# Copies of packed queries and keys issued earlier on the SP queue, in a gated attention and mixture-of-experts layer

## The chip, the cores and the metric

The kernel runs on one core of one Trainium2 chip. The metric is the device time of one execution in microseconds. Three runs of the kernel before took 1435.66, 1438.06 and 1438.19 us; their median is 1438.06 us. The core has a TensorE (PE, matmuls), a VectorE (DVE), a ScalarE (ACT) and a GpSimd (POOL), which work side by side and wait for one another by semaphores, and SP, which here does nothing but issue copies (DMAs).

## The reference

The layer is a cross-attention with a gate, followed by a mixture of experts with a gate. The change is in the attention.

```python
# B=16 batches, N=256 tokens, M=1601 context rows, D=128, H=16 heads of 8
def _L0_xattn_ref(q, k, v, Wq, Wk, Wv, Wo):
    qh = jnp.einsum('bnd,hde->bhne', q, Wq)
    kh = jnp.einsum('bmd,hde->bhme', k, Wk)
    vh = jnp.einsum('bmd,hde->bhme', v, Wv)
    scores = jnp.einsum('bhne,bhme->bhnm', qh, kh) * SCALE
    att = jax.nn.softmax(scores, axis=-1)
    out_h = jnp.einsum('bhnm,bhme->bhne', att, vh)
    ...
x = x + jnp.tanh(g_xattn[0]) * _L0_xattn_ref(_layernorm(x), ctx_1024, ctx_1024, ...)
x = x + jnp.tanh(g_ffn[0]) * _L0_ffn_ref(_layernorm(x), ...)   # 8 experts, top 2
```

## The kernel before

The attention goes through the 16 batches, one after the other. A batch has 4 groups of 4 heads, and a group has 13 tiles of up to 128 context rows (the last has 65). One tile of one group is a *unit*; a batch has 52 units, r = 0 to 51, and every engine's program is written as a loop over all 832 units, in which r decides what is done besides.

In each unit TensorE makes the scores of its tile (L716, `st`), ScalarE takes their exponentials (L1022), and TensorE multiplies those of two units ago with the values (L759, `pv`). The softmax needs the maximum of each query's scores beforehand. For that TensorE computes the scores a second time in *windows* of 402 context rows (L738, `mxp`), VectorE reduces each window (L1456, `mx`), GpSimd splits the maxima in three bf16 terms (L610 to L616), TensorE turns them (L773), ScalarE copies them to `mxT` (L1077), and SP copies them into three rows of `qpack` (L427, `place_maxima`). From there the matmul of the scores subtracts them. The windows run ahead: at the start of a batch 28 of its 64 windows are done, and the first window of the *next* batch is issued in unit 27.

Queries and keys are float32, but are multiplied as bf16: each number is split into three bf16 terms (`qsp`, `ksp`), and six products of terms are stacked in the rows of `qpack` and `kpack`. The stacking is what SP's copies do:

- `pack_queries(b)` (L379) is 12 copies of 32 KB: 6 parts, each for 2 row groups;
- `pack_keys(b, g)` (L373) is 12 copies of 50 KB for one group of heads, so 48 a batch.

`qpack` and `kpack` each have two halves; batch b uses half b % 2. So the packs of batch b + 1 wait until all scores of batch b - 1 are done (`s_st`), and until the terms are there (`s_q3`, `s_k3`).

SP's program is one queue: what stands behind a wait or behind other copies goes later. In the loop of batch b it holds, in this order of units: 9 (maxima of group 1; queries of b + 1; keys of b + 1, group 0), 23 (maxima of group 2; keys of groups 1 and 2), 35 (maxima of group 3; keys of group 3; load of a context), 48 (maxima of group 0 of the next batch). SP itself does not follow the units. It runs on to its next wait, and the only waits of the loop that hold it for long are those for `mxT`.

At the turn of two batches GpSimd issues the four scatters of token rows for the experts (L644, `write_rows`), and TensorE begins with the key projection of the next batch (L818, in units 1, 2, 3 and 6). Values are projected in units 13, 14, 27 and 32 (L827). After the last batch come the experts: 39 blocks of 256 tokens, whose results are scattered by GpSimd (L652).

Of the kernel before, what the change touches and what calls it, by code (L numbers as in the profile page):

```python
# [16 lines left out]
B, N, D = 16, 256, 128  # L17
# [32 lines left out]
PARTS = len(K_KIND)  # L50
# [140 lines left out]
def build(nc, x, ctxT, gates, wq, wk, wv, woT, rwT, w1T, w2T, ident, tables, pads, out):  # L191
# [4 lines left out]
    with ctx:  # L196
# [173 lines left out]
        def pack_key_rows(eng, b, g, part, rg):  # L370

            p0 = rg * RSTEP
            eng.dma_start(kpack[p0 + part:p0 + MAXROW:PARTS, b % 2, g * JJ:(g + 1) * JJ, 0:M],  # L373
                          ksp[p0 + g:p0 + RSTEP:NG, K_KIND[part], 0:M]
                          ).then_inc(s_kd[b % 2][g], 16)

        def pack_query_rows(eng, b, part, rg):
            r = rg * RSTEP
            eng.dma_start(qpack[r + part:r + MAXROW:PARTS, b % 2, :, :],  # L379
                          qsp[r:r + RSTEP, Q_KIND[part], :]).then_inc(s_qd[b % 2], 16)  # L380
# [16 lines left out]
        def _(eng):  # L397
# [5 lines left out]
            def pack_keys(b, g, kinds=range(PARTS)):  # L403

                if g == 0:
                    eng.wait_ge(s_k3, NK * (b + 1))
                    if b > 1:
                        eng.wait_ge(s_st, RG * UNITS * (b - 1))
                for part in kinds:
                    for rg in range(RG):  # L410
                        pack_key_rows(eng, b, g, part, rg)

            def pack_queries(b):
                eng.wait_ge(s_q3, b + 1)
                if b > 1:
                    eng.wait_ge(s_st, RG * UNITS * (b - 1))
                for part in range(PARTS):
                    for rg in range(RG):
                        pack_query_rows(eng, b, part, rg)

            def place_maxima(G):
                b, g = divmod(G, NG)
                eng.wait_ge(s_mxT, G + 1)
                rows = KINDS * JJ
                for rg in range(RG):
                    r = rg * RSTEP + MAXROW
                    eng.dma_start(qpack[r:r + KINDS, b % 2, g * JJ:(g + 1) * JJ, :],  # L427
                                  mxT[rg * rows:(rg + 1) * rows, :]).then_inc(s_mxd[G % 2], 16)

            def load_context(b):  # L430
                if b + 2 < B:
                    eng.wait_ge(s_v, NV * (b + 1))
                    eng.dma_start(ctx_sb[:, b % 2, :], ctxT[b + 2]).then_inc(s_ctx[b % 2], 16)
# [22 lines left out]
            for u in range(B * UNITS):  # L456
                b, r = divmod(u, UNITS)
                if u == 20:
                    eng.dma_start(rows[NE * CAP:NE * CAP + SPARE * SL, :], pads[NE * 2 * SL:PADS, :]
                                  ).then_inc(s_pad, 16)  # L460
                if r in PLACE_AT and b * NG + PLACE_AT[r] < GROUPS:
                    place_maxima(b * NG + PLACE_AT[r])
                if b == 0:
                    if r == 9:
                        pack_queries(1)
                    elif r == 23:
                        pack_keys(1, 0)
                        pack_keys(1, 1)
                    elif r == 35:
                        pack_keys(1, 2)  # L470
                        pack_keys(1, 3)
                        load_context(1)
                elif b + 1 < B:
                    if r == 9:
                        pack_queries(b + 1)
                        pack_keys(b + 1, 0)
                    elif r == 23:
                        pack_keys(b + 1, 1)
                        pack_keys(b + 1, 2)
                    elif r == 35:  # L480
                        pack_keys(b + 1, 3)
                        load_context(b + 1)
# [1215 lines left out]
```

## Time and profile before

| | |
|---|---|
| median of 3 runs | 1438.06 us (1435.66 to 1438.19) |
| the profiled execution | 1438.06 us, its span 1436.2 us |
| granted TensorE clock, mean | 0.966 |
| TensorE, VectorE, ScalarE, GpSimd busy | 93%, 82%, 77%, 38% |
| SP's key packs, query packs, maxima | 762, 186 and 128 copies |
| one batch of the attention | about 74 us |

The profile is that of one execution. A page gives the busy time of each engine, the chain of work that ended last, and groups of instructions by line. Queries of the trace behind it give, for a stretch of time, every instruction of an engine, what it waited for, and the share of time for which the DMA engines were busy. Names are those of the program: `qpack<-qsp` is a copy from `qsp` to `qpack`. An engine's idle time counts only if the engine is on the chain that sets the end.

### The profile page before, as it was taken

Reading aid. Unit: us, or ns where it says so; the run is one execution under the profiler, and the core shown is the slowest. Engines: PE = TensorE matmul, PEld = TensorE weight load, DVE = VectorE, ACT = ScalarE, POOL = GpSimd, SP = SyncE. Lnnn points to the kernel's source line nnn. Section 1 sums busy time; section 2 is a strip of 40 time slices with the busy share of each in tenths; the row PEclk is TensorE's granted clock in tenths of the full one; section 3 lists DMA queues with packets and bytes.
Section 4 is the critical chain, followed back from the end, with each engine's and each line's share of the span. In section 5 each row is a group of like instructions: output and inputs, shape, how many; then the busy total and the mean of one; then the engine's idle time right before and its main releaser. Section 6 shows DMA issues by size and latency. Waiting matters only on the chain.

```text
span 1436.2 us, 37917 instructions
## 1 busy us (share of the span) xinstructions
PE 1339.1 (93%) x13936; PEld 651.0 (45%) x13936; DVE 1171.2 (82%) x2302; ACT 1100.8 (77%) x2202; POOL 545.2 (38%) x1213
## 2 busy tenths in 40 slices
PE   4689999999999999999999999999999999998993
PEld 2233444444444444444444443434444433486882
DVE  6777898989898989898989898989999998253444
ACT  1467898888888979797988888888888888764551
POOL 1231525262625253435353535343434312144442
PEclk7698999999999999999999999999999999899996
DMA  3422121212121212121212121212111110375665
GB/s 87 149 65 63 30 77 38 77 36 78 33 81 28 74 35 71 38 69 42 67 44 65 47 64 50 62 52 56 59 53 38 49 43 2 108 226 173 205 208 197
DMA packets 65556, 109.15 MB, mean 76 GB/s; under 512 B 13452, under 2 KB 36364, under 8 KB 65228
## 3 DMA queue, kind: packets, MB, share of 16 engines
q1 hardware_dynamic: 56716, 92.46, 21.9%
q0 software_dynamic: 4544, 9.45, 2.0%
q10 hardware_dynamic: 4112, 4.83, 1.0%
q8 instruction: 111, 1.82, 0.5%
q14 instruction: 73, 0.60, 0.1%
HBM read 48.81 MB, written 14.64 MB: 44 GB/s over the span
## 4 chain that ended last, share of the span: by engine, by line
PE 80%; DVE 10%; issue 3%; another core or an unknown queue 2%; SPq 1%; DMA 1%; ACT 1%; ACTq 1%; POOL 0%; POOLq 0%; DVEq 0%
PE pv L759 28%; PE mxp L738 15%; PE st L716 14%; DVE mx L1456 9%; PE st L983 5%; PE mxp L993 5%; PE st L827 4%; PE st L818 3%; PE st L838 2%; SPq L373 1%; PE st L790 1%; PE st L861 1%; PE st L802 1%; ACT arena L1022 1%
## 5 line engine op out<-in xcount | busy, mean ns | idle before, releaser
L1456 DVE TENSOR_REDUCE mx<-mxp 128x2 f32<-128x804 f32 x1024 | 987.5, 989 | 118.7 <-PE mxp L738 81.9
L1022 ACT ACTIVATE arena<-st 128x512 f32<-128x512 f32 (+1 forms) x1664 | 898.6, 594 | 145.9 <-PE st L716 118.6
L759 PE MATMUL pv<-arena 128*32 128x256 f32 x6656 | 538.2, 395 | 12.9 <-issue 12.2
L738 PE MATMUL mxp<-kpack,qpack 48*128 48x402 bf16 x2048 | 455.5, 344 | 34.4 <-DVE mx L1456 20.6
L716 PE MATMUL st<-qpack,kpack 51*128 51x256 bf16 (+1 forms) x3328 | 459.3, 274 | 11.3 <-issue 10.2
L716 PEld LDWEIGHTS st<-qpack,kpack 51*128 51x128 bf16 (+1 forms) x3328 | 207.2, 97 | 216.7 <-ACT arena L1022 110.6
L738 PEld LDWEIGHTS mxp<-kpack,qpack 48*128 48x128 bf16 x2048 | 139.5, 94 | 177.9 <-DVE mx L1456 85.8
L759 PEld LDWEIGHTS pv<-arena 128*32 128x32 f32 x6656 | 132.5, 108 | 191.4 <-issue 100.2
L610 POOL CAST mxs<-nmx 128x8 bf16<-128x8 f32 x64 | 12.1, 189 | 323.1 <-DVE nmx L1464 323.1
L1162 ACT ACTIVATE arena<-st,bias 128x256 f32<-128x256 f32 x156 | 73.5, 474 | 64.2 <-PE st L983 43.3
L652 POOL DMA_INDIRECT results<-ysb,idx x78 | 74.8, 959 | 106.3 <-DVE ysb L1588 93.8
L983 PE MATMUL st<-xT,arena 128*128 128x256 f32 x312 | 94.9, 387 | 6.5 <-ACT xT L1150 6.1
L644 POOL DMA_INDIRECT rows<-xrow,pos x64 | 63.9, 998 | 92.4 <-DVE pos L1345 77.4
L536 POOL TENSOR_TENSOR tmp<-rstd 128x2 f32<-128x2 f32 x93 | 18.0, 193 | 208.1 <-DVE rstd L1218 203.2
L993 PE MATMUL mxp<-arena 128*128 128x256 f32 x312 | 93.9, 384 | 0.0
L1588 DVE TENSOR_SCALAR ysb<-mxp,xblk,tgate 128x128 f32<-128x128 f32 x78 | 28.4, 405 | 48.2 <-PE mxp L967 44.0
L818 PE MATMUL st<-arena,wk_sb 128*128 128x400 f32 (+1 forms) x126 | 62.0, 578 | 5.2 <-DMA arena<-in_ctxT 5.2
L993 PEld LDWEIGHTS mxp<-arena 128*128 128x128 f32 x312 | 60.1, 193 | 8.4
L827 PE MATMUL st<-wv_sb,arena 128*128 128x128 f32 (+1 forms) x416 | 62.2, 289 | 0.0
L827 PEld LDWEIGHTS st<-wv_sb,arena 128*128 128x128 f32 (+1 forms) x416 | 49.6, 187 | 25.1 <-issue 24.6
L983 PEld LDWEIGHTS st<-xT,arena 128*128 128x128 f32 x312 | 53.6, 193 | 12.0 <-ACT xT L1150 6.7
L585 POOL TENSOR_TENSOR ksp<-kf,ksp 128x400 bf16<-128x400 f32 (+1 forms) x60 | 56.8, 947 | 4.8
(183 smaller groups left out, 976.6 us busy)
## 6 DMA issues: line engine op xcount, KB each, us to landing
kpack<-ksp SPq DMA_DIRECT2D x762, 50.0 KB
arena<-in_ctxT SPq DMA_DIRECT2D x15, 800.5 KB, 4.4
arena<-in_w1T SPq DMA_DIRECT2D x39, 256.0 KB
arena<-in_w2T SPq DMA_DIRECT2D x39, 256.0 KB
qpack<-qsp SPq DMA_DIRECT2D x186, 32.0 KB
xblk<-rows SPq DMA_DIRECT2D x39, 132.0 KB
rows<-in_pads SPq DMA_DIRECT2D x8, 264.0 KB
qpack<-mxT SPq DMA_DIRECT2D x128, 3.0 KB
```

What stands on the lines that cost most here:

```text
L644: eng.indirect_dma_start(rows, bass.IndirectOffsetOnAxis(ap=pos[:, k, t:t + 1].bitcast(U32), axis=0), xrow[:, t, k, :], None).then_inc(don ...
L652: eng.indirect_dma_start(results, bass.IndirectOffsetOnAxis(ap=idx[:, i % IDX_BUFS, j:j + 1].bitcast(U32), axis=0), ysb[:, i % YS_BUFS, j, ...
L716: ins = eng.matmul(ring[i][0:n, jj * N:(jj + 1) * N], kpack[rows, b % 2, g * JJ + jj, kt * P:kt * P + n], qpack[rows, b % 2, g * JJ + jj, ...
L738: eng.matmul(mxp[pair % MX_BUFS][:, rg, 0:WIN], qpack[rows, b % 2, g * JJ + jj, t * P:(t + 1) * P], kpack[rows, b % 2, g * JJ + jj, WSTART ...
L759: ins = eng.matmul(pv[32 * j:32 * j + 32, 0:N], vaug[0:n, b % 2, kt, VC * h:VC * h + 32], pt[0:n, (2 * u + rg) % PT_BUFS, jj * N:(jj + 1) ...
L818: eng.matmul(dst[:, 0:kn], wk_sb[:, :], ctx_sb[:, b % 2, k0:k0 + kn], start=True, stop=True).then_inc(s_kp, 1)
L827: ins = eng.matmul(ring[i][0:n, t * D:(t + 1) * D], ctx_sb[:, b % 2, (t0 + t) * P:(t0 + t) * P + n], wv_sb[:, :], start=True, stop=True)
L983: eng.matmul(hp[q % HP_BUFS][:, 0:SL], wbuf[:, i % W_BUFS, 0, c * P:(c + 1) * P], xT[:, i % 2, :], start=True, stop=True).then_inc(s_hp, 1)
L993: eng.matmul(yp[i2 % 2][:, 0:SL], wbuf[:, i2 % W_BUFS, 1, c2 * P:(c2 + 1) * P], hf[:, f % RING, :], start=(c2 == 0), stop=(c2 == HC - 1)). ...
L1022: eng.activation(pt[0:n, c % PT_BUFS, :], ring[bank_of["S", u, p]][0:n, :], ACT.Exp, scale=SCALE).then_inc(s_exp, 1)
L1162: eng.activation(hf[:, q % RING, :], hp[q % HP_BUFS][:, 0:SL], ACT.Gelu_apprx_tanh, bias=bias[:, i % BIAS_BUFS, c:c + 1]).then_inc(s_hg, 1)
L1456: eng.tensor_reduce(mx[:, tj, w, :], mxp[windows_done % MX_BUFS][:, :, 0:WIN], AX.X, ALU.max).then_inc(s_red, 1)
```

## The change

In the loop of SP the query packs of the next batch move from unit 9 to unit 1, which also puts them ahead of the maxima of group 1. This holds for the batches b = 1 to 14; batch 0 keeps its order. The twelve key packs of group 1 are cut in two: the first three parts (6 copies) are issued at unit 16, the other three at unit 23 as before. No other engine's program changes, and no wait is added or removed; the waits of `pack_queries` move with it.

```diff
@@ -458,6 +458,8 @@
                 if u == 20:
                     eng.dma_start(rows[NE * CAP:NE * CAP + SPARE * SL, :], pads[NE * 2 * SL:PADS, :]
                                   ).then_inc(s_pad, 16)
+                if r == 1 and 0 < b < B - 1:
+                    pack_queries(b + 1)
                 if r in PLACE_AT and b * NG + PLACE_AT[r] < GROUPS:
                     place_maxima(b * NG + PLACE_AT[r])
                 if b == 0:
@@ -472,10 +474,11 @@
                         load_context(1)
                 elif b + 1 < B:
                     if r == 9:
-                        pack_queries(b + 1)
                         pack_keys(b + 1, 0)
+                    elif r == 16:
+                        pack_keys(b + 1, 1, range(PARTS // 2))
                     elif r == 23:
-                        pack_keys(b + 1, 1)
+                        pack_keys(b + 1, 1, range(PARTS // 2, PARTS))
                         pack_keys(b + 1, 2)
                     elif r == 35:
                         pack_keys(b + 1, 3)
```

On SP's queue before, one batch of the steady state stands as follows, from the context load at the end of one batch to the next. The first row `qpack<-mxT` is the maxima of group 0 and of group 1.

```order
L433 DMA arena<-in_ctxT 128x1601
L427 DMA qpack<-mxT 3x2x256 x4
L379 DMA qpack<-qsp 8x8x256 x12
L373 DMA kpack<-ksp 8x2x1601 x12
L427 DMA qpack<-mxT 3x2x256 x2
L373 DMA kpack<-ksp 8x2x1601 x24
L427 DMA qpack<-mxT 3x2x256 x2
L373 DMA kpack<-ksp 8x2x1601 x12
```

The same stretch of SP's queue in the changed kernel:

```order
L433 DMA arena<-in_ctxT 128x1601
L427 DMA qpack<-mxT 3x2x256 x2
L379 DMA qpack<-qsp 8x8x256 x12
L427 DMA qpack<-mxT 3x2x256 x2
L373 DMA kpack<-ksp 8x2x1601 x18
L427 DMA qpack<-mxT 3x2x256 x2
L373 DMA kpack<-ksp 8x2x1601 x18
L427 DMA qpack<-mxT 3x2x256 x2
L373 DMA kpack<-ksp 8x2x1601 x12
```

The query packs now stand between the maxima of group 0 and those of group 1, and the 12 and 24 key packs around the maxima of group 2 have become 18 and 18.

## Rows read from the trace of the kernel before

**Rows 1.** The page, part 1: busy time of each engine.
```profile
PE 1339.1 (93%) x13936; PEld 651.0 (45%) x13936; DVE 1171.2 (82%) x2302; ACT 1100.8 (77%) x2202; POOL 545.2 (38%) x1213
```
**Rows 2.** The page, part 4: the chain that ended last, by engine.
```profile
PE 80%; DVE 10%; issue 3%; another core or an unknown queue 2%; SPq 1%; DMA 1%; ACT 1%; ACTq 1%; POOL 0%; POOLq 0%; DVEq 0%
```
**Rows 3.** Tile qpack: releaser of its matmuls, us idle in total, times.
```profile
  DMA qpack<-mxT: 2.7, 6
```
**Rows 4.** Waits: engine, line, releaser, total us, times, longest us.
```profile
PE mxp L738 <- DMA qpack<-qsp: 8.6, 1, 8.6
```
**Rows 5.** Timeline of SP from 520 us: start, us, line, copy, count.
```profile
526.68 1.43 SPq L427 DMA_DIRECT2D qpack<-mxT  x2
528.22 7.90 SPq L379 DMA_DIRECT2D qpack<-qsp  x12
536.22 7.79 SPq L373 DMA_DIRECT2D kpack<-ksp  x12
...
546.08 1.51 SPq L427 DMA_DIRECT2D qpack<-mxT  x2
547.64 15.67 SPq L373 DMA_DIRECT2D kpack<-ksp  x24
```
**Rows 6.** Stretches: us, engines' busy time, PEclk, DMA share, GB/s.
```profile
512.00:515.00 3.00, 2.06 (x19) 0.93 (x18) 0.34 (x2) 1.33 (x4) 2.34 (x4) 1.00 0.18 58
...
528.00:536.00 8.00, 8.00 (x94) 4.46 (x95) 7.04 (x16) 6.37 (x13) 0.00 (x0) 1.00 0.18 45
...
545.00:547.60 2.60, 2.60 (x35) 1.40 (x27) 2.44 (x4) 2.14 (x5) 0.00 (x0) 1.00 0.01 1
```
**Rows 7.** Timeline of TensorE at the batch's turn and in unit 27.
```profile
508.27 0.27 PE L716 MATMUL st<-qpack,kpack 51*65 51x256 bf16 x1
...
553.05 0.34 PE L738 MATMUL mxp<-kpack,qpack 48*128 48x402 bf16 x2
```
**Rows 8.** Timeline of GpSimd: the query terms, first and last of four scatters.
```profile
500.64 0.67 POOL L598 TENSOR_TENSOR qsp<-qf,qsp 128x256 bf16<-128x256 f32 x1
...
509.02 1.10 POOL L644 DMA_INDIRECT rows<-xrow,pos  x1 [5.46 <-DVE pos L1345]
...
512.97 0.97 POOL L644 DMA_INDIRECT rows<-xrow,pos  x1 [0.30 <-issue]
```
**Rows 9.** Timeline of VectorE: idle us and releaser in brackets.
```profile
514.80 1.90 DVE L1456 TENSOR_REDUCE mx<-mxp 128x2 f32<-128x804 f32 x2 [2.66 <-remote]
```
**Rows 10.** The chain in order of time at the start of batch 6: start, us.
```profile
512.14 2.68 another core or an unknown queue
```
**Rows 11.** Timeline of SP: the maxima of group 0, start of a period.
```profile
283.34 22.25 SPq L427 DMA_DIRECT2D qpack<-mxT  x4
...
356.78 22.99 SPq L427 DMA_DIRECT2D qpack<-mxT  x4
...
430.98 22.99 SPq L427 DMA_DIRECT2D qpack<-mxT  x4
```
**Rows 12.** Timeline of ScalarE and SP: mxT and the late maxima of batch 5.
```profile
487.95 0.36 ACT L1077 ACTIVATE mxT<-st 12x256 bf16<-12x256 f32 x1
...
489.97 1.51 SPq L427 DMA_DIRECT2D qpack<-mxT  x2
...
526.30 0.36 ACT L1077 ACTIVATE mxT<-st 12x256 bf16<-12x256 f32 x1
```
**Rows 13.** Timeline of TensorE's weight loads: waits for maxima, batches 5, 10.
```profile
492.59 0.09 PEld L716 LDWEIGHTS st<-qpack,kpack 51*128 51x128 bf16 x1 [0.41 <-DMA qpack<-mxT]
...
863.19 0.09 PEld L716 LDWEIGHTS st<-qpack,kpack 51*128 51x128 bf16 x1 [0.58 <-DMA qpack<-mxT]
```
**Rows 14.** The page, parts 2 and 5: DMA by slices; scatters, mean ns.
```profile
DMA  3422121212121212121212121212111110375665
...
L652 POOL DMA_INDIRECT results<-ysb,idx x78 | 74.8, 959 | 106.3 <-DVE ysb L1588 93.8
L644 POOL DMA_INDIRECT rows<-xrow,pos x64 | 63.9, 998 | 92.4 <-DVE pos L1345 77.4
```

## The prediction

> **What bounds the kernel now.** I read the busy shares first [rows 1]: TensorE has work for 93% of the span, VectorE for 82%, ScalarE for 77%. The chain of waits [rows 2] agrees: 80% of the span is TensorE's, 10% VectorE's, and DMA and the SP queue have 1% each. So the span is set by TensorE, and the change touches only the order in which SP issues copies. It can matter in three ways: a wait of a computing engine on one of those copies goes or comes; a copy behind them on SP moves; or the copies meet other traffic at a bad place. I went through them in this order.
>
> First, who waits for the copies at all. The tile view of qpack and the table of waits answer: over the whole run TensorE was idle 2.7 us in six waits for the maxima [rows 3], and once, for 8.6 us, for query packs [rows 4]. A wait that comes once in 16 batches is that of the start, where nothing runs ahead, and the packs of batch 0 are not moved. No wait for kpack stands in either view.
>
> Second, how late the packs are. Batch 6 (from about 509 to 583 us) stands for the steady state. SP issues the 12 query packs from 528.22, the first 12 key packs from 536.22 to 544.01 [rows 5]. From 545.0 on the DMA share is 0.01 [rows 6], so the last key pack of group 0 has landed by about 545.5. The first window of the next batch is the matmul at 553.05, behind the value projection of L827 [rows 7]. The slack is 7.5 us before the change.
>
> Third, what else happens at the place to which the query packs go. On SP the packs will stand behind the group-0 maxima, and then wait for the last scores of the batch before. Those are the 65-row matmuls that end at 508.54 [rows 7]. So the packs will be issued from about 508.6. In exactly that stretch GpSimd issues four scatters of token rows, 509.02 to 513.94 [rows 8], and in exactly that stretch all three computing engines stand still: VectorE waits 2.66 us [rows 9], and the chain has 2.68 us of "another core or an unknown queue" [rows 10]; from 512 to 515 VectorE works 0.34 us and ScalarE 1.33 us [rows 6]. Batches come in two lengths, and this stop is where they differ. From the SP rows: 356.78 - 283.34 = 73.44 us and 430.98 - 356.78 = 74.20 us [rows 11], 0.76 us apart. By the same rows nine of the batches 2 to 14 are of the long kind and four of the short one. This is the only part of the loop where I find anything to win or to lose.
>
> **The change part by part.** The profiled execution took 1438.06 us (span 1436.2, 1.9 us around it). That is the median of the three runs as well, so the sum is made against 1438.06.
>
> (a) Query packs of batches 2 to 15 move from unit 9 to unit 1 of the batch before, ahead of the maxima of group 1. Twelve packs with their gaps take 7.90 us [rows 5]: 508.6 + 7.9 = 516.5. The next copy on SP is the group-1 maxima, issued at 526.68 right behind mxT at 526.30 + 0.36 [rows 5, 12]. SP is free 10 us before that, so this copy is not delayed: cost 0. The new wait on s_st stands in front of the same copy only, and is over at 508.54: cost 0. The split queries it reads are finished by GpSimd at 500.64 + 0.67 [rows 8]. What the packs free later: the first key packs go from 536.22 to about 528.2, and slack grows from 7.5 to 15.5 us. It was not used, so 0.
>
> (b) Half of the group-1 key packs (3 of 6 parts, each for two row groups, so 6 of 12 copies) go ahead of the maxima of group 2: 6 x 0.65 = 3.9 us. With (a) SP runs 528.2 + 7.8 + 3.9 = 540 us, and the group-2 maxima are due at 546.08 [rows 5]. 6 us of slack, cost 0. Without (a) the six would end at 548 and push the maxima by 2 us; (a) is the cover of (b).
>
> (c) Behind the group-2 maxima stand now 18 packs instead of 24: 18 x 0.653 = 11.8 us instead of 15.67. The group-3 maxima are free to go at 547.64 + 11.8 = 559.4 and wait for mxT instead of for SP. In a batch such as batch 5, SP took 16.44 us for the 24 and issued the maxima at 489.97, while mxT was there at 487.95 + 0.36 = 488.31: 1.66 us late [rows 12]. TensorE's weight load then names this copy, but it is idle 0.41 us there, which is what it is idle in the neighbouring units as well; only in batch 10 is it 0.58 [rows 13]. The gain is 0.58 - 0.41 = 0.17 us once. The bound from above is the whole 2.7 us of [rows 3].
>
> (d) The last twelve key packs and the context load of each batch go earlier by at most 15.67 - 11.8 = 3.9 us. Nobody waits for either: 0.
>
> (e) The meeting with the scatters. No row of before shows the two together in the loop. Bounds: below, that the stop becomes short everywhere, 9 batches x 0.76 us = -7 us. Above: the query packs hold the DMA engines for a share of 0.18 over 8 us [rows 6], 1.44 us of each engine; if the stop grew by all of that in the 13 batches that have both, +18.7 us. The nearest rows speak for a value near 0: the scatters of the tail (results), issued where the last digits of the page's DMA line show 30 to 79% busy, take 959 ns on GpSimd; those of the loop (rows), with next to no other traffic, 998 ns [rows 14]. I take 0.
>
> The Trainium skill ("DMA: Bandwidth & Descriptors", section "Issuing engines are not separate DMA queues") says that copies started by sync and by gpsimd run on the same 16 DMA engines and interleave, whoever starts them. That rule speaks against this change, which puts twelve packs onto the engines that have to carry the scatters; that the scatters wait for it is not shown by any run here. By it the sum would be the rival below, 1444; by the GpSimd durations it is the forecast.
>
> Sum: 1438.06 - 0.17 + 0 = **1437.9 us**.
>
> **The rivals.**
> Rival 1, slower: the scatters' data wait behind the packs, and the stop that ends with them grows. Twelve packs hold each engine 1.44 us, 0.12 us each on the mean; four scatters that each meet one add 0.5 us to the stop, in 13 batches 6 us: 1444. For it: the stop lies exactly under the scatters, in a batch with scatters and with nothing else on the queues (DMA share 0.18 between 512 and 515 [rows 6]). Against it: the GpSimd durations above. It decides from 0.22 us per batch.
>
> Rival 2, faster: the stop is short instead of long. Long and short batches start with the same order, so something small decides; a shift by the packs may bring all to the short kind: 1438.06 - 7 = 1431. Against: nothing says that the shift goes this way.
>
> Rival 3, the reverse: the four short batches become long, 4 x 0.76 = +3: 1441.
>
> Rival 4, the change does not do what it says: the packs "at unit 16" follow the packs of unit 9 on SP with no wait between, so nothing is held until unit 16, and the time is the forecast's.
>
> **How the numbers follow.** What a measurement can tell from no change here is about 0.2%, 2.9 us. Forecast (with rival 4) 0.48, own range 1436 to 1440. Rival 1 0.24, rival 2 0.17, rival 3 0.11. Rival 2 is faster by over 0.2%, with 0.05 of the forecast's case that the stop shifts partly to the short kind: faster 0.22. Rival 1 in all and half of rival 3 are slower: 0.30. Same is the rest, 0.48. The 8-in-10 range takes in rival 2, rival 3 and most of rival 1: 1431 to 1446.
>
> **What would show it.** (a) SP's query packs at the start of each batch, 20 us before the group-1 maxima, and these right behind mxT. (b), (c) 18 packs on either side of the group-2 maxima, the group-3 maxima always right behind mxT, and no six waits of L716 on them. (e) The stop: VectorE's idle time before the windows behind the scatters (2.66 us in batch 6) and the batch periods of 73.4 and 74.2 us. If the periods are the old two in about the old numbers, the forecast is right for its reason. If all are 74.6 and over it is rival 1, if all are 73.4 rival 2. The forecast would be wrong too if the first windows of a batch (L827 ahead of them) waited for DMA, or if the maxima of group 1 were issued later than mxT.

## The result, and the profile after

The changed kernel took 1470.88 us (median of 4 runs, 1470.43 to 1476.03); the kernel before took 1438.12 us (median of 4, 1435.66 to 1441.16). The ratio is 1.0235, 95% interval 1.0205 to 1.0265: the change made the kernel slower by 33 us. The forecast was 1437.9 us, its range ended at 1446.

The profiled execution of the changed kernel was its fastest: 1459.57 us, span 1457.8 us, mean granted clock 0.954. The other four ran at 0.946 to 0.949. So the trace shows 21.5 us of the loss, against 1438.06 us of before. The run of 1470.63 us lost 11 us more; its clock (0.949 over a span of 1468.8 us) accounts for at most 7.8 us of them.

The page after, part 1 and the chain by engine of part 4 (they answer to [rows 1, 2]):

```profile
PE 1354.1 (93%) x13936; PEld 653.0 (45%) x13936; DVE 1171.7 (80%) x2302; ACT 1103.3 (76%) x2202; POOL 548.0 (38%) x1213
...
PE 82%; DVE 9%; issue 3%; another core or an unknown queue 3%; DMA 1%; ACT 1%; ACTq 1%; POOL 0%; POOLq 0%; SPq 0%; DVEq 0%
```

The instruction counts are the same. The span grew by 1457.8 - 1436.2 = 21.6 us. TensorE's busy time grew by 1354.1 - 1339.1 = 15.0 us, that is, the same matmuls took longer; the other 6.6 us are time in which it stood. The granted clock bears this out: 1457.8 x (1 - 0.954) - 1436.2 x (1 - 0.966) = 18.2 us of the full clock were lost in addition, which is the most that the clock can have cost. VectorE's busy time did not grow (1171.2 before).

SP, changed kernel: start, us, line, copy, count. The first rows are the turn to batch 5.

```profile
286.81 7.90 SPq L379 DMA_DIRECT2D qpack<-qsp  x12
...
361.40 7.90 SPq L379 DMA_DIRECT2D qpack<-qsp  x12
...
432.50 1.51 SPq L427 DMA_DIRECT2D qpack<-mxT  x2
436.01 7.90 SPq L379 DMA_DIRECT2D qpack<-qsp  x12
457.00 1.52 SPq L427 DMA_DIRECT2D qpack<-mxT  x2
458.63 11.76 SPq L373 DMA_DIRECT2D kpack<-ksp  x18
...
513.14 7.90 SPq L379 DMA_DIRECT2D qpack<-qsp  x12
587.74 9.12 SPq L379 DMA_DIRECT2D qpack<-qsp  x12
```

The queue does what the order said: the query packs at the turn, 18 key packs in a piece where 12 and 24 stood. The packs also mark the batches, since they wait for the last scores of the batch before: 74.59, 74.61, 77.13 and 74.60 us from one to the next. Before, the two lengths were 73.44 and 74.20 [rows 11]. So these batches are 0.4 us longer than the old long kind, and one is 2.9 us longer.

Where that is: at the turn, under the scatters. GpSimd, VectorE and the chain of the changed kernel at the turn to batch 5 (start, us, then the instruction, with its idle us and their releaser in brackets; the chain has start, us, and what held it):

```profile
436.36 1.11 POOL L647 DMA_INDIRECT rows<-xrow,pos  x1 [5.46 <-DVE pos L1348]
...
440.32 0.97 POOL L647 DMA_INDIRECT rows<-xrow,pos  x1 [0.31 <-issue]
```

```profile
438.56 0.99 DVE L1459 TENSOR_REDUCE mx<-mxp 128x2 f32<-128x804 f32 x1 [0.57 <-PE mxp L741]
442.56 1.90 DVE L1459 TENSOR_REDUCE mx<-mxp 128x2 f32<-128x804 f32 x2 [3.01 <-remote]
...
449.52 1.00 DVE L1459 TENSOR_REDUCE mx<-mxp 128x2 f32<-128x804 f32 x1 [2.35 <-PE mxp L741]
```

```profile
439.30 1.76 another core or an unknown queue
...
441.20 1.26 another core or an unknown queue
...
443.05 1.70 PE st L821 x2
```

The scatters are as long and as far apart as before [rows 8] (509.02 to 512.97 there, 436.36 to 440.32 here: 3.95 and 3.96 us). VectorE's wait in the middle of them is 3.01 us instead of 2.66 [rows 9], the nameless piece of the chain 1.76 + 1.26 = 3.02 us instead of 2.68 [rows 10]. TensorE had computed the window by then:

```profile
439.39 0.56 PE L741 MATMUL mxp<-kpack,qpack 48*128 48x402 bf16 x4
...
441.57 0.64 PE L762 MATMUL pv<-arena 128*32 128x256 f32 x8 [1.25 <-issue]
```

```profile
439.00:442.00 3.00, 1.75 (x18) 0.60 (x16) 0.55 (x1) 1.18 (x3) 1.94 (x2) 1.00 0.42 103
442.00:445.00 3.00, 2.15 (x10) 0.63 (x6) 2.14 (x4) 1.69 (x4) 1.79 (x3) 0.64 0.25 63
445.00:449.00 4.00, 4.00 (x23) 1.52 (x20) 1.90 (x2) 1.74 (x4) 3.55 (x9) 0.50 0.02 6
```

TensorE works 1.75 us of 3, then 2.15 of 3, and then the granted clock is at 0.50, the lower of its two levels (1.2 GHz), while it works without a pause: 23 matmuls in 4 us, with VectorE (1.90) and ScalarE (1.74) half idle behind it. That is the second wait of 2.35 us at 449.52. In the changed kernel's trace this happens behind the turn of eight batches (5, 9 to 15); in the one of before it happens at no turn of batches 2 to 15.

Measured from first scatter to first scatter, batches 2 to 14 take 982.51 us together, against 959.97 before, 22.5 us more. The six batches without a fall (2 to 4, 6 to 8) have 3.6 us of this, 0.6 us each; the seven with one (5, 9 to 14) have 18.9 us. The eighth fall, at the turn to batch 15, comes where no query packs are issued, behind a VectorE wait of 1.26 us, and the stretch from there to the next scatters is only 0.5 us longer than before.

Two stretches of 15 us over a turn, with the fall (batch 5) and without it (batch 8), both from some 2 us ahead of the first scatter:

```profile
434.00:449.00 15.00, 12.90 (x107) 4.75 (x100) 8.99 (x15) 8.91 (x18) 9.36 (x15) 0.79 0.18 46
660.00:675.00 15.00, 12.76 (x132) 4.74 (x124) 10.93 (x17) 10.88 (x22) 9.19 (x15) 1.00 0.18 46
```

TensorE is as busy in both, and gets 107 matmuls done in the one and 132 in the other.

### The profile page after: what moved, and what is told of

It is laid out like the page before. It is cut to its first block, busy times and chain, and to the rows that moved or that the text cites. A ratio compares the mean times of both kernels' runs of the same rounds, so it can differ in the third digit from the quotient of the medians.

```text
span 1457.8 us, 37917 instructions
## 1 busy us (share of the span) xinstructions
PE 1354.1 (93%) x13936; PEld 653.0 (45%) x13936; DVE 1171.7 (80%) x2302; ACT 1103.3 (76%) x2202; POOL 548.0 (38%) x1213
## 4 chain that ended last, share of the span: by engine, by line
PE 82%; DVE 9%; issue 3%; another core or an unknown queue 3%; DMA 1%; ACT 1%; ACTq 1%; POOL 0%; POOLq 0%; SPq 0%; DVEq 0%
PE pv L762 29%; PE st L719 15%; PE mxp L741 15%; DVE mx L1459 8%; PE st L986 5%; PE mxp L996 4%; PE st L830 4%; PE st L821 4%; PE st L841 2%; PE st L793 1%; DMA arena<-results 1%; PE st L864 1%; PE st L805 1%; PE mxp L962 1%
## 5 line engine op out<-in xcount | busy, mean ns | idle before, releaser
L741 PE MATMUL mxp<-kpack,qpack 48*128 48x402 bf16 x2048 | 461.6, 348 | 29.0 <-DVE mx L1459 14.4
L986 PE MATMUL st<-xT,arena 128*128 128x256 f32 x312 | 94.4, 386 | 6.1 <-ACT xT L1153 5.7
L647 POOL DMA_INDIRECT rows<-xrow,pos x64 | 64.1, 1001 | 92.3 <-DVE pos L1348 77.4
L821 PE MATMUL st<-arena,wk_sb 128*128 128x400 f32 (+1 forms) x126 | 69.7, 643 | 12.6 <-ACT kf L1056 6.5
L1056 ACT ACTIVATE kf<-st 128x400 f32<-128x400 f32 (+1 forms) x60 | 30.4, 507 | 40.6 <-PE st L821 30.8
```

The source lines that it names most:

```text
L647: eng.indirect_dma_start(rows, bass.IndirectOffsetOnAxis(ap=pos[:, k, t:t + 1].bitcast(U32), axis=0), xrow[:, t, k, :], None).then_inc(don ...
L741: eng.matmul(mxp[pair % MX_BUFS][:, rg, 0:WIN], qpack[rows, b % 2, g * JJ + jj, t * P:(t + 1) * P], kpack[rows, b % 2, g * JJ + jj, WSTART ...
L821: eng.matmul(dst[:, 0:kn], wk_sb[:, :], ctx_sb[:, b % 2, k0:k0 + kn], start=True, stop=True).then_inc(s_kp, 1)
L986: eng.matmul(hp[q % HP_BUFS][:, 0:SL], wbuf[:, i % W_BUFS, 0, c * P:(c + 1) * P], xT[:, i % 2, :], start=True, stop=True).then_inc(s_hp, 1)
```

## The experiments

Two things had to be told apart: what lengthens the stop, and what of it is the clock. The theory (M) was that the query packs cost because they meet the four scatters; rivals were that they cost by themselves at that place (Q), and that the stop belongs to the turn of the batches and not to the scatters (S). Each group of runs had its own runs of the kernel before on the same chip, and its ratio is to these. The table gives the median, the ratio with its interval, and from each profile the span and TensorE's busy and idle time (the span less the busy time), since idle time shows roughly the stops and busy time roughly the clock. The medians of the kernel before in these groups were 1428.64 us (runs 1 to 4), 1428.79 (5 to 7), 1437.60 (8 to 11) and 1435.48 (12). Of these no trace was kept, so the rows of before are always those of the profiled 1438.06 us; for runs 1 to 7, whose kernel before was some 9.5 us faster, small differences to these rows may be the chip's.

| kernel | us | ratio | span | busy | idle |
|---|---|---|---|---|---|
| before | 1438.12 | 1 | 1436.2 | 1339.1 | 97.1 |
| changed | 1470.88 | 1.0235 [1.0205, 1.0265] | 1457.8 | 1354.1 | 103.7 |
| 1 queries only | 1465.02 | 1.0241 [1.0205, 1.0276] | 1467.2 | 1363.5 | 103.7 |
| 2 key cut only | 1447.90 | 1.0117 [1.0085, 1.0150] | 1450.3 | 1346.8 | 103.5 |
| 3 changed, packs behind scatters | 1429.47 | 0.9992 [0.9974, 1.0010] | 1425.6 | 1337.2 | 88.4 |
| 4 before, scatters later | 1449.26 | 1.0162 [1.0117, 1.0206] | 1442.5 | 1347.2 | 95.3 |
| 5 changed, scatters later | 1493.12 | 1.0453 [1.0435, 1.0471] | 1493.3 | 1370.7 | 122.6 |
| 6 before + twelve small copies | 1461.48 | 1.0225 [1.0200, 1.0250] | 1461.5 | 1358.6 | 102.9 |
| 7 before + one large copy | 1430.58 | 1.0023 [1.0000, 1.0046] | 1432.4 | 1338.0 | 94.4 |
| 8 before, scatters spread | 1410.32 | 0.9794 [0.9755, 0.9833] | 1411.0 | 1334.1 | 76.9 |
| 9 changed, scatters spread | 1409.00 | 0.9784 [0.9745, 0.9824] | 1410.2 | 1333.7 | 76.5 |
| 10 as 3, scatters spread | 1409.84 | 0.9781 [0.9736, 0.9827] | 1409.4 | 1332.2 | 77.2 |
| 11 before + six small copies | 1472.76 | 1.0236 [1.0192, 1.0280] | 1469.5 | 1365.7 | 103.8 |
| 12 changed, scatters in pairs | 1415.39 | 0.9854 [0.9812, 0.9895] | 1416.9 | 1339.6 | 77.3 |

**1. The query packs alone.** The changed kernel without the cut of the key packs:

```diff
-                    elif r == 16:
-                        pack_keys(b + 1, 1, range(PARTS // 2))
                     elif r == 23:
-                        pack_keys(b + 1, 1, range(PARTS // 2, PARTS))
+                        pack_keys(b + 1, 1)
```

> The changed kernel without the cut of the key packs: the query packs stay at unit 1, the 12 key packs of group 1 go back behind the maxima of group 2. Theory M (the loss is the meeting of the query packs with GpSimd's four scatters at the turn of the batches, which lengthens the stop there and lets TensorE's clock fall): 1471 us, as the changed kernel, within 5 us. Rival K (the cut of the key packs at unit 16 costs): 1438 us, as before.

Ratio 1.0241, the whole loss (1465 us is 6 below the 1471 that M named, beside a kernel before that is 9.5 us faster). VectorE at the turn to batch 4 shows both waits, 3.00 us and, after the fall of the clock, 2.26 us:

```profile
371.99 1.90 DVE L1457 TENSOR_REDUCE mx<-mxp 128x2 f32<-128x804 f32 x2 [3.00 <-remote]
...
378.43 1.00 DVE L1457 TENSOR_REDUCE mx<-mxp 128x2 f32<-128x804 f32 x1 [2.26 <-PE mxp L739]
```

**2. The key cut alone.** The kernel before with the same lines the other way round (query packs stay at unit 9).

> The kernel before with only the cut of the key packs (query packs at unit 9 as before). M: 1438 us, at most 2 us more, since the maxima of group 2 then wait about 2 us on SP and may reach their scores late. K: 1471 us.

Ratio 1.0117, far more than expected: a miss for the size. The place is as the prediction had it: without the early query packs, the six key packs push the group-2 maxima. SP, ScalarE and the weight loads of TensorE in batch 6:

```profile
541.71 11.70 SPq L373 DMA_DIRECT2D kpack<-ksp  x18
553.46 1.51 SPq L427 DMA_DIRECT2D qpack<-mxT  x2
```

```profile
551.19 0.36 ACT L1079 ACTIVATE mxT<-st 12x256 bf16<-12x256 f32 x1
```

```profile
556.09 0.09 PEld L718 LDWEIGHTS st<-qpack,kpack 51*128 51x128 bf16 x1 [1.18 <-DMA qpack<-mxT]
```

mxT is there at 551.55, the copy starts at 553.46, 1.9 us late, and TensorE stands 1.18 us. All waits for these copies sum to 35.9 us in 27 times (before: 2.7 in 6 [rows 3]). In batch 3 the wait is 2.37 us, and the clock falls behind it:

```profile
329.09 0.09 PEld L718 LDWEIGHTS st<-qpack,kpack 51*128 51x128 bf16 x1 [2.37 <-DMA qpack<-mxT]
```

```profile
328.00:332.00 4.00, 2.91 (x29) 0.99 (x29) 2.33 (x7) 2.21 (x5) 0.07 (x1) 0.79 0.22 61
332.00:340.00 8.00, 8.00 (x54) 3.75 (x56) 4.97 (x14) 4.27 (x9) 0.72 (x4) 0.50 0.28 80
```

So the fall needs no scatters; it comes behind a stop of TensorE from another cause as well. In the changed kernel this loss does not exist: no wait for `qpack<-mxT` stands in the view of this tile any more.

**3. The packs a little later.** The changed kernel, with one wait more on SP, so that the packs go out when the scores of unit 5 are done:

```diff
                 if r == 1 and 0 < b < B - 1:
+                    eng.wait_ge(s_st, RG * (b * UNITS + 6))
                     pack_queries(b + 1)
```

> The changed kernel with one wait more on SP: the query packs wait for the scores of unit 5 of their batch, some 11 us into it, when the scatters are over, and still stand ahead of the maxima of group 1. M: 1438 us (1435 to 1441), the stop back at 2.7 us of VectorE idle time or less, and no fall of the clock between 147 us and the end of the attention. Rival Q (the packs cost what they do wherever they run beside the first units of a batch and the key projection, scatters or not): 1450 us or more.

Ratio 0.9992: the loss is gone, with the packs still ahead of the group-1 maxima and the key cut in place. The turn to batch 4, VectorE and SP:

```profile
361.62 1.90 DVE L1460 TENSOR_REDUCE mx<-mxp 128x2 f32<-128x804 f32 x2 [1.90 <-PE mxp L742]
```

```profile
293.88 7.90 SPq L379 DMA_DIRECT2D qpack<-qsp  x12
...
367.21 7.90 SPq L379 DMA_DIRECT2D qpack<-qsp  x12
```

The wait is shorter than the 2.66 us of before, and the batch (367.21 - 293.88 = 73.33 us) is of the short kind; whether the kernel before had the short kind on this chip too is not known. Q falls: the same packs in the same order cost nothing 11 us later, behind the scatters. One detail of the expectation failed: the clock fell once within the attention, behind the turn to batch 15 (1172 to 1176 us at 0.57), where no packs are issued. The changed kernel's fall at the same turn therefore need not be the packs' doing either.

**4. The scatters later.** The kernel before, with the four scatters of a batch issued behind the split of the next batch's keys:

```diff
+                    if b > 1:
+                        write_rows(b - 2, s_sc)
                     norm("L", b - 1)
...
                     count_second(b - 1)
-                    write_rows(b - 1, s_sc)
+            write_rows(B - 2, s_sc)
```

> The kernel before, with GpSimd's four scatters of a batch moved behind the split of the next batch's keys, some 17 us later; the packs are where they were, so that the scatters now meet the first query packs at about unit 14. M says that the stop belongs to the scatters: units 0 to 2, now 7.7 us in a long batch, get 3 to 3.5 us shorter, and the stop comes back where the scatters now are, longer than it was, since packs are issued there too: 1435 to 1475 us. Rival S (the stop belongs to the turn of the batch, its key projection and copies, and the scatters only lie beside it): units 0 to 2 keep their 7.7 us.

Ratio 1.0162. At the turn nothing is left of the stop, and it is where the scatters now are (GpSimd issues them at 379.89 to 383.85). VectorE of this kernel in batch 4:

```profile
366.04 1.90 DVE L1458 TENSOR_REDUCE mx<-mxp 128x2 f32<-128x804 f32 x2 [0.92 <-PE mxp L740]
...
386.08 1.00 DVE L1458 TENSOR_REDUCE mx<-mxp 128x2 f32<-128x804 f32 x1 [1.30 <-remote]
```

The stop belongs to the scatters (S falls). That moving it made the kernel slower fits what SP does there: it issues the maxima at 377.92 and the query packs from 379.46, beside the scatters.

**5. Both changes.** The changed kernel with the scatters of run 4.

> The changed kernel, and besides the four scatters of each batch are issued by GpSimd later, behind the split of the next batch's keys, as in the earlier run (there the stop went with them to units 11 and 12). The query packs are then alone at the turn, at 5 to 13 us of the batch. Theory M (the packs cost by meeting the scatters): the turn is as short as with the scatters moved alone (units 0 to 2 about 5.4 us), no clock fall there; what is left is the stop at units 11 and 12, which now meets the first key packs or the maxima of group 1: 1445 to 1455 us. If the packs cost by themselves at the turn, units 0 to 3 stay above 7.7 us and the time is 1465 or more.

The turn is as M says, 0.92 us. The size is a miss: 1493 us instead of at most 1455. Four scatters now start within the 18 key packs, and this is the worst meeting of all. VectorE and SP of batch 4, and the stretches:

```profile
372.46 1.90 DVE L1461 TENSOR_REDUCE mx<-mxp 128x2 f32<-128x804 f32 x2 [0.92 <-PE mxp L743]
...
392.69 0.99 DVE L1461 TENSOR_REDUCE mx<-mxp 128x2 f32<-128x804 f32 x1 [3.63 <-remote]
```

```profile
386.15 11.76 SPq L373 DMA_DIRECT2D kpack<-ksp  x18
```

```profile
390.00:394.00 4.00, 0.61 (x6) 0.23 (x10) 1.31 (x3) 1.35 (x3) 0.97 (x1) 0.67 0.39 116
394.00:398.00 4.00, 4.00 (x24) 2.44 (x24) 1.23 (x3) 1.40 (x4) 0.00 (x0) 0.50 0.30 83
```

**6, 7 and 11. Number or data?** Prediction and rival 1 both priced the packs by the share of the DMA engines that they hold. The kernel before got, at the place of the early query packs, twelve copies of 4 KB (6), six of them (11), or one of 393 KB, the data of all twelve packs (7), in batches 1 to 14. Nobody reads what they write. The diff is that of run 6; run 11 has `range(6)`, and run 7 has `eng.dma_start(spare, x[0:768, :])` in place of the loop:

```diff
+                if r == 1 and 0 < b < B - 1:
+                    eng.wait_ge(s_st, RG * UNITS * b)
+                    if b > 1:
+                        eng.wait_ge(s_dum, 16 * 12 * (b - 1))
+                    for n in range(12):
+                        eng.dma_start(spare[16 * n:16 * (n + 1), :],
+                                      ident[16 * (n % 8):16 * (n % 8 + 1), 0:64]).then_inc(s_dum, 16)
```

> The kernel before, and besides SP issues twelve copies of 4 KB (16 rows of 256 bytes from a constant on the chip to a spare DRAM tensor) where the changed kernel has the query packs, in batches 1 to 14. So the number of issues is that of the query packs and the data next to nothing. Theory N (the number of copies issued beside the scatters lengthens the stop): +0.4 us or more in the turns of 13 batches and clock falls behind some, 1440 us or more, against some 1429 to 1438 of before. Theory V (the data on the DMA engines does): as before within 3 us.

> The kernel before, and besides SP issues at the same place one copy of 393 KB (DRAM to DRAM), as much data as the twelve query packs in one issue. Theory V (the data on the DMA engines lengthens the stop): a turn longer by 0.4 us or more in 13 batches, with clock falls, 1440 us or more. Theory N (the number of issues): as before within 3 us.

> The kernel before with six of the small copies at the turn instead of twelve (twelve: 1461.5 us, one large copy: 1430.6). If the stop grows with the number of copies issued beside the scatters, it is between: a turn longer by 0.2 to 0.4 us, and fewer falls of the clock, 1435 to 1450. If twelve are needed to reach the last of the scatters' completions, it is as before; if the first few do all of it, 1458 or more.

Ratios 1.0225, 1.0023 and 1.0236. The twelve small copies make the loss of the change, the one large copy with as much data makes hardly any, and six small ones are enough. (In run 6 SP and VectorE, then in run 7, then in run 11, all at the turn to batch 4.)

```profile
360.88 7.92 SPq L467 DMA_DIRECT2D spare<-in_ident  x12
```

```profile
367.50 1.90 DVE L1464 TENSOR_REDUCE mx<-mxp 128x2 f32<-128x804 f32 x2 [2.96 <-remote]
```

```profile
359.15 0.58 SPq L466 DMA_DIRECT2D spare<-in_x  x1
```

```profile
365.30 1.90 DVE L1463 TENSOR_REDUCE mx<-mxp 128x2 f32<-128x804 f32 x2 [2.64 <-remote]
```

```profile
363.58 4.11 SPq L467 DMA_DIRECT2D spare<-in_ident  x6
```

```profile
370.04 1.90 DVE L1464 TENSOR_REDUCE mx<-mxp 128x2 f32<-128x804 f32 x2 [2.75 <-remote]
```

2.96 us is close to the 3.01 of the changed kernel, 2.64 to the 2.66 of before. Batch 4 is not typical of run 11: over batches 3 to 14 its waits are 2.75 to 3.05 us, ten of twelve above 2.9, and those of run 6 are 2.77 to 3.16. So the stop is as long with six copies as with twelve, and the time lies above the 1435 to 1450 that was expected for a cost that grows with the number: the third case of that expectation, "the first few do all of it". The six are issued in the first 4.1 us, just while the scatters are. In run 7 five of the turns to batches 3 to 14 have the long stop (2.61 to 2.64 us) and the others a shorter one. Its data runs early: the DMA share is 0.88 in the us from 360 and 0.44, 0.39 and 0.21 in the next three, while the scatters are issued from 359.55 to 364.45 (in the changed kernel it is some 0.4 from 363 to 368). So this run alone doesn't clear the data beside the last scatters. Runs 6 and 11 do: the loss comes with 48 and 24 KB. What they share with the change is that several copies are started beside the scatters. The small copies also have short rows (256 bytes); the query packs, with long ones, do the same harm, so that is not the cause either.

**8, 9 and 10. One scatter at a time.** Before (8), changed (9) and run 3's kernel (10), each with the four scatters apart, between the splits of the next batch's keys and maxima (shortened: `scatter`, one pass of the loop of `write_rows`, is left out, and so are the conditions of the four calls, b > 1):

```diff
+                    scatter(b - 2, 0)
                     if b + 1 < B:
                         split_keys(b + 1, 0)
+                    scatter(b - 2, 1)
                     split_maxima(b * NG + 1)
+                    scatter(b - 2, 2)
                     if b + 1 < B:
+                        split_keys(b + 1, 1)
+                    scatter(b - 2, 3)
+                    if b + 1 < B:
-                        for c in range(1, NK):
+                        for c in range(2, NK):
```

> The kernel before, with the four scatters of a batch no longer in a row: GpSimd issues them one by one in the next batch, ahead of and between the splits of the keys and of the maxima, with 2 us or more of other work between two of them. Theory R (a single scatter holds TensorE's completions back by some tenths of a us, and the stop comes of several in a row): no stop of 2 us anywhere, units 0 to 2 at 5.4 us as when all four are moved, and nothing like the 2.78 + 2.63 us at units 11 and 12: 1405 to 1420 us where before is 1428.6. Theory T (each scatter holds them by the same amount wherever it stands): the sum stays, 1425 to 1435, or up to 1449 as with all four moved if the clock falls.

> The changed kernel with its early query packs and its cut of the key packs, and the scatters spread as in the run beside it. If the loss of the change is only the query packs' meeting with four scatters in a row (theory R), it is gone, and the time is within 5 us of the kernel with spread scatters alone. If single scatters beside copies of SP hold TensorE too, it stays 10 us or more above that one. With all four in a row at units 11 to 13 the changed kernel took 1493.

> The kernel in which the query packs of the change wait until unit 6's scores begin (1429.5 us), with the scatters spread as well. By theory R, as fast as spread scatters alone, 1405 to 1420, or faster by the one or two us that the group 3 maxima no longer wait; by theory T 1425 to 1450.

Ratios 0.9794, 0.9784 and 0.9781: all three beat the kernel before by 2.1%, and the three are not to be told apart. The change costs nothing here although its twelve packs start right beside the first scatter. SP, GpSimd, VectorE and the stretches of run 9:

```profile
287.52 7.90 SPq L379 DMA_DIRECT2D qpack<-qsp  x12
...
359.34 7.90 SPq L379 DMA_DIRECT2D qpack<-qsp  x12
```

```profile
359.69 1.10 POOL L657 DMA_INDIRECT rows<-xrow,pos  x1 [5.46 <-DVE pos L1369]
```

```profile
363.13 1.90 DVE L1480 TENSOR_REDUCE mx<-mxp 128x2 f32<-128x804 f32 x2 [0.89 <-PE mxp L762]
```

```profile
361.00:364.00 3.00, 3.00 (x33) 1.03 (x29) 2.11 (x3) 2.60 (x7) 0.52 (x2) 1.00 0.28 68
```

The updates of the matmuls for which VectorE waits here stand 0.01 to 0.05 us behind their ends (363.06 and 363.23), where they were 2.6 to 2.8 us late in the changed kernel; the 0.89 us is the wait for the matmuls themselves. TensorE works 3.00 us of 3 with a DMA share of 0.28. The expectation of run 8 put 2 us or more of other work between two scatters; in run 9's trace they start at 359.69, 366.70, 368.91 and 373.25, so the smallest gap holds 1.2 us of work. Only the first two meet the packs (359.34 to 367.24). A batch takes 359.34 - 287.52 = 71.82 us: 1.62 less than the short kind of before. In run 8 (without the change) one batch is long, far from the scatters: the group-3 maxima, which still stand behind 24 key packs there, came late for once, TensorE stood 2.06 us, and the clock fell:

```profile
482.37 1.51 SPq L427 DMA_DIRECT2D qpack<-mxT  x2
```

```profile
485.00 0.28 PE L737 MATMUL st<-qpack,kpack 51*128 51x256 bf16 x1 [2.06 <-DMA qpack<-mxT]
```

```profile
483.00:486.00 3.00, 1.00 (x14) 0.45 (x14) 0.94 (x3) 0.89 (x3) 0.00 (x0) 1.00 0.13 37
486.00:490.00 4.00, 4.00 (x34) 1.24 (x30) 2.89 (x7) 3.13 (x8) 0.00 (x0) 0.56 0.30 83
```

**12. Two at a time.** The changed kernel with one pair of scatters ahead of the first key split and one pair behind the maxima.

> The changed kernel with the scatters in two pairs, one pair at the turn beside the query packs, one behind the first split of the keys. With single scatters it took 1409.0 us beside a before of 1437.6 (ratio 0.978) and its first unit 1.24 us; batch 15 of that run has a pair at its turn without packs, and its first unit takes 1.66 us. If a pair holds TensorE a little and packs beside it little more: 0.4 to 1 us per batch, ratio 0.982 to 0.990. If a pair is enough for the stop and the clock falls that four bring: ratio 1.00 or more. If it takes three: as with single ones, 0.978.

Ratio 0.9854, in the first of the three bands. A batch takes 360.39 - 288.08 = 72.31 us by the packs, 0.49 more than with single scatters, and the clock falls at no turn. In its trace 5.9 of the 6.7 us of span more than run 9's are in TensorE's busy time (1339.6 against 1333.7), with the mean clock as in run 9 (0.967 and 0.965), so the table's split into stops (idle) and clock (busy) is only a rough one. Two pairs cost something, four in a row three to five times as much: 73.44 - 71.82 = 1.62 or 74.20 - 71.82 = 2.38 us before.

## Why the prediction was wrong

The step that failed is (e), "The meeting with the scatters", where the text says "The nearest rows speak for a value near 0 ... I take 0". The term measured +33 us by the medians (+21.5 in the trace). Both its value and its upper bound (+18.7) were wrong, for two reasons.

First, the rows chosen could not show the cost. 959 and 998 ns [rows 14] are the time for which GpSimd is busy with issuing a scatter. In the changed kernel that is still 1001 ns, and the scatters stand where they stood. The cost is with TensorE, whose finished matmuls reach VectorE and ScalarE late while scatters are issued in a row. Neither does the bound by the DMA share (1.44 us a batch) measure it: run 7 puts as much data there for 2 us between the medians (3 by the ratio), runs 6 and 11 put next to none there for 33 and 35 us.

Second, the stop was priced as time standing and nothing else. By the two pages the standing grew by 6.6 us, some 0.5 us a turn in 13 turns; by the batches without a fall it is 0.6 us a turn. The rest, 15.0 us of longer matmuls, is for the most part the clock (18.2 us at most; an estimate by batches gives 18.9 - 7 x 0.6 = 14.7), and it was more in the runs at a mean clock of 0.946 to 0.949. In the trace of before the stop passes at full clock [rows 6] at every turn from batch 2 on, so nothing in the sum had a term for the lower level. This is the term that was missing.

Point by point:

(a) Right as far as it goes. The query packs start 21 us ahead of the group-1 maxima, and these go out at 457.00, right behind mxT (456.62 + 0.36). The cost of the place they moved to was put under (e).

(b) Right, and its cover was worth more than stated. "Without (a) the six would end at 548 and push the maxima by 2 us" is run 2: 1.9 us late in batch 6. What was not priced is what such a push would do: 1.17% of the time.

(c) Right: the waits of the weight loads for `qpack<-mxT` went from 2.7 us to none. It is too small to be measured here.

(d) Right: the table of waits shows none for key packs, and one for a context, at the start.

Rival 1 had the place, and its 0.5 us a batch is the growth of the standing (6 us, 6.6 measured). Its mechanism was another: runs 6 and 11 lose the same with next to no data for the scatters' data to wait behind. Its price lacked the clock. The rule cited, that copies of all starters share and interleave on the same 16 DMA engines (the Trainium skill, "DMA: Bandwidth & Descriptors", section "Issuing engines are not separate DMA queues"), is not at odds with any run; what I drew from it, that bytes would be the price, is.

Rival 2 had the wrong sign: the stop did not become short anywhere in batches 2 to 14. Rival 3 happened as a part of the larger effect: a short batch of 73.44 us became one of 74.59. The prediction's count of nine long batches is one more than have the long stop: in the trace of before VectorE waits 2.66 to 2.69 us at eight turns (to batches 4 to 9, 11 and 12) and 1.3 to 2.0 us at the other six. Rival 4 changes nothing, as said.

What stays open is the path on which the news of TensorE is delayed. The runs show that it takes several scatters in a row, that several copies started beside them lengthen it, and that it does not take their bytes. The Trainium skill ("DMA: Bandwidth & Descriptors", section "Why a DMA increments its semaphore by 16 and not by 1") says that every DMA engine which takes part in a copy ends it with a write of its own to the semaphore. By that, twelve copies bring about twelve times the writes of one large copy, which agrees with runs 6 and 7; six copies would bring half of them, and run 11 shows no less harm. No run here separates these writes from the making of descriptors or other work that each copy needs, so it stays a guess. Open, too, is why one stop of some 3 us is followed by the lower clock and another is not (batches 3, 4 and 6 to 8 of the changed kernel were spared with waits of 2.85 to 3.03 us), and why the clock falls at the turn to batch 15 in the traces of runs 1, 3, 6, 7 and 11 and the changed kernel, where SP issues nothing at the turn.

## What to carry to other kernels

Before a copy is moved to a quiet place on its queue, look at what other starters do there: beside a row of GpSimd scatters a handful of copies costs as much as a dozen, whatever they carry, and the scatter's own duration does not show it. When all engines stand still for a "remote" or "unknown" reason, move or spread what is issued under it, before anything around it is tuned: here that was worth 2.1%, while the change itself was expected to win 0.17 us. And where TensorE sits near full load, price a stop twice, once as time and once with the lower clock behind it.

## What the runs showed of the hardware

- Four scatters of 128 rows each, issued in a row, hold back the news of TensorE's finished matmuls. The semaphore updates stand 2.2 us behind the matmuls' modelled ends in the kernel before and 2.6 to 2.8 us with packs beside the scatters, but 0.01 to 0.05 us at the same place of run 9, whose single scatters start 2.2 us or more apart. VectorE waits 2.66 us [rows 9], 3.01 us and 0.89 us. A batch is 1.62 to 2.38 us shorter with single ones, 0.49 us less so with two pairs.
- Copies started by SP beside the four scatters lengthen VectorE's wait, at most 2.69 us before, to 2.75 to 3.05 us (six of 4 KB) or 2.77 to 3.16 us (twelve) in batches 3 to 14, and bring falls of the clock; one copy of 393 KB leaves it at 2.64 us or less.
- The granted clock went to 0.50 behind stops of different causes: scatters (changed kernel, busy 1.75 of 3 us before the fall), a late copy of maxima (run 8, busy 1.00 of 3 us; run 2, busy 2.91 of 4). In batch 5 the stretch at the lower clock made the batch 2.5 us longer than its neighbours (77.13 against 74.60).
